# First steps of three stages moved ahead of their stage: embedding spreads, second attention, mixture gate

## The chip, the core and the metric

One Trainium2 chip, of which the kernel uses one core: TensorE (PE; PEld is its weight load), VectorE (DVE), ScalarE (ACT), GpSimd (POOL) and SyncE (SP, which only issues transfers here). Each engine runs its own instruction list in order; the lists meet at semaphores. The metric is the device time of one execution in microseconds (us), the median of several runs. In the rows, L12 is line 12 of the kernel, and a clock of 1.0 or 0.5 is TensorE's granted clock at its full level or at half of it.

## The reference

32 sequences of 512 tokens, width 64. An embedding, then four residual blocks, each on a layer norm of the running state:

```python
h = tok_ref(x, token_W, pe)                      # table row + position row; positions skip pads after a separator
h = h + attn0(layernorm(h), Wq, Wk)              # softmax(q k^T / 8) x, no value or output weights
h = h + ffn0(layernorm(h), route_id, ...)        # 64 -> 128, two layers of shared + routed expert, -> 64
h = h + attn1(layernorm(h), Wq, bq, ..., Wo, bo) # attention with all weights
h = h + ffn1(layernorm(h), Wg, ...)              # 8 experts of 64 -> 128 -> 64 with GELU, sum of the top 2
```

## The kernel before

The state `H` stays on chip for all 32 sequences. A stage handles one sequence per step, with double buffers (`par` is the step's parity), and the stages follow each other: embedding, attention `a0`, routed stage `f0`, attention `a1`, mixture `f1`. Every engine has its own sweep over the sequences; the order of the work on an engine is that of its code, written by hand.

**Embedding.** Token ids become one-hot matrices. On PE `spread_ids(i)` (L909, one 512-column product) spreads the ids of sequence i into bank 2 or 3; DVE compares them with a column (`one_hots`, tile OH, L638). For each four sequences `spread_pos` (L917) and OP (L634) do it for positions. `embed(i)` on PE (L939, L941) is 24 small products of the one-hots with the tables `T3`, each table kept as three bf16 parts; ACT copies the sum to `H` (L413). `embed(i)` waits for OH(i), and behind its products it issues `spread_ids(i + 2)`. DVE has other work between its one-hots: `low_weights` behind sequence 15, `products` behind 20, and a layer norm's statistics (`first_norms`) behind 14, 17, 20, 23 and 26. Ahead of all this, DVE works out positions (L604 to L616), splits the tables into `T3` (L620 to L626), and then spreads the positions (PDX, L589).

**Attention.** For a sequence: PE makes `project` (L1013, L1014) from the turned input X2; ACT copies it (QH, L481); DVE keeps the low part (`low_parts`, Q2, L737); PE makes four 128x512 tiles of scores only to find row maxima (`scores_for_max`, L1024), DVE reduces them (`maxima`, L743); PE spreads the maxima into a row (`spread_max`, L1037), ACT copies it (L497), PE makes the scores again (L1049, L1050), ACT takes exp (L504), PE multiplies with the values (L1058), ACT copies (OT, L475), PE turns back (`turn_back`, L996), and DVE divides and adds to `H` (`finish`, L750 to L754). Inside the sweep, project and maxima of the next sequence run ahead; for sequence 0 they stand ahead of the sweep, one behind the other, and in `a1` behind waits for the routed stage's last step:

```python
if before is not None:
    pe.wait_ge(before.h0_ready, NSEQ)
    pe.wait_ge(before.h1_ready, NSEQ)
    pe.wait_ge(before.h2_ready, NSEQ)
project(0, 0)
...
    rest_before()          # a1: leave0(31), turn_back(31) of the routed stage
for t in range(NT):
    scores_for_max(0, 0, t)
```

**Routed stage.** Per sequence: `enter0` (L1119, L1120), `routed` layer 0 and layer 1 (L1135), with relu on ACT (L530) and on DVE (`layer1`, L797), `leave0` (L1144), a copy on ACT (L473), `turn_back` (L1003) and `add_back` on DVE (L805). The steps of a sequence are spread over several sweep steps, so that after the sweep a tail of layer 1, leave0 and turn_back for the last sequences is left.

**Mixture.** Gate products (`gate_scores`, L1183), the top two on DVE (`copy_xh` L872, `gate_sum` L836 to `gate_masks` L862), turned masks (`turn_masks`, L1190), copied by ACT (`masks`, L547); then eight up products (L1206, L1207), GELU on ACT (L556), and down products (L1226). For sequence 0 the gate's products stand in the last step of `a1`'s sweep, ahead of its values; the choice on DVE (`first_gate`) behind that step's statistics; in the first attention the same two places hold the routed stage's `enter0(0)` and `experts_of(0)`; `turn_masks(0)` on PE and `masks(0)` on ACT behind the attention.

## Time and profile before

| | us |
|---|---|
| median of 3 runs | 935.1 (934.78 to 936.87) |
| the profiled execution | 936.95 |
| span of its instructions | 935.1 |
| PE busy in the span | 891.6 (95%) |
| DVE, ACT, POOL busy | 603.8, 576.6, 384.1 |

The profile was taken in one further execution. Busy times are sums over the span; a PE that is busy may run at half its clock. The stages by the trace: embedding products from 15.3 to 64.6 us, first attention to 287, routed stage to 407, second attention to 632, mixture to the end.

### The profile page before, as it was taken

How to read it: one execution, taken by the hardware profiler on the slowest of the kernel's cores; microseconds unless marked ns; L12 is line 12 of the kernel's file. 1: busy time of each engine (PE TensorE's matmuls, PEld its weight loads, DVE VectorE, ACT ScalarE, POOL GpSimd, SP SyncE). 2: the span in 40 equal slices, each digit the busy share in tenths (PEclk: the TensorE clock that was granted, in tenths of full speed). 3: DMA queues.
4: the chain of work that ended last, by engine and by line, in shares of the span. 5: the costliest groups of instructions: out<-in, count | busy, mean ns of one | idle time of the engine just before them, and what ended most of it. 6: DMA issues, size and time to landing. Idle time of an engine off the chain costs nothing.

```text
span 935.1 us, 21847 instructions
## 1 busy us (share of the span) xinstructions
PE 891.6 (95%) x6198; PEld 631.5 (68%) x6198; DVE 603.8 (65%) x2610; ACT 576.6 (62%) x1195; POOL 384.1 (41%) x523
## 2 busy tenths in 40 slices
PE   4879999999999999979999999999999999999998
PEld 2657666666766676656666676666777777777775
DVE  5876777778787899967777777774434343434321
ACT  1336666666666666646666666666666666666664
POOL 0133444444437888834444344443333333333300
PEclk9999999999999999989999999999999999999999
DMA  4000000000001222200000000000000000000000
GB/s 103 2 1 2 1 0 0 0 0 0 1 1 49 72 73 68 75 7 1 1 0 0 0 0 1 1 1 7 12 18 11 17 11 17 11 17 11 18 13 23
DMA packets 18995, 15.13 MB, mean 16 GB/s; under 512 B 5762, under 2 KB 18946, under 8 KB 18946
## 3 DMA queue, kind: packets, MB, share of 16 engines
q1 hardware_dynamic: 18946, 14.52, 5.6%
q8 instruction: 26, 0.43, 0.2%
q14 instruction: 23, 0.19, 0.1%
HBM read 10.32 MB, written 4.19 MB: 16 GB/s over the span
## 4 chain that ended last, share of the span: by engine, by line
PE 83%; DVE 12%; issue 2%; ACT 1%; DMA 1%; DVEq 0%; POOL 0%; SPq 0%; ACTq 0%
PE bank L1226 13%; PE bank L1058 13%; PE bank L1206 7%; PE bank L1024 7%; PE bank L1207 6%; PE bank L971 5%; DVE nmax L743 5%; PE bank L1049 5%; PE bank L1050 5%; PE bank L1135 4%; PE bank L996 3%; PE bank L1037 2%; PE bank L1013 2%; PE bank L1014 2%; PE bank L1003 2%
## 5 line engine op out<-in xcount | busy, mean ns | idle before, releaser
L743 DVE TENSOR_REDUCE nmax<-bank 128x1 fp32r<-128x512 f32 x256 | 170.4, 687 | 47.7 <-PE bank L1024 47.5
L360 POOL TENSOR_TENSOR XS<-XN,XS 128x252 fp32r<-128x252 f32 x128 | 98.0, 765 | 211.6 <-ACT XS L402 211.6
L342 POOL TENSOR_TENSOR rstd<-VE,half 128x4 f32<-128x4 f32 x128 | 129.2, 1009 | 119.6 <-DVE VE L661 119.6
L504 ACT ACTIVATE PT<-bank 128x512 f32<-128x512 f32 x256 | 146.0, 596 | 41.8 <-PE bank L1050 35.5
L354 POOL TENSOR_TENSOR XN<-XC,rstd 128x252 f32<-128x252 f32 x128 | 78.3, 612 | 183.9 <-PE bank L1058 183.7
L556 ACT ACTIVATE PT<-bank 128x512 f32<-128x512 f32 x256 | 132.2, 605 | 3.5 <-PE bank L1207 2.8
L475 ACT ACTIVATE OT<-bank 128x256 f32<-128x256 f32 x96 | 36.8, 384 | 154.3 <-PE bank L1058 103.8
L1058 PE MATMUL bank<-PT,XN 128*64 128x256 f32 x1024 | 124.7, 386 | 0.0
L1226 PE MATMUL bank<-PT,W 128*64 128x256 f32 x1024 | 124.5, 386 | 0.0
L1024 PE MATMUL bank<-X,QH 128*128 128x512 f32 x256 | 108.2, 424 | 8.6 <-DVE nmax L743 1.7
L1049 PE MATMUL bank<-QH,X 128*128 128x512 f32 x256 | 113.1, 442 | 0.5 <-ACT Q L497 0.5
L453 ACT ACTIVATE X<-bank 128x512 fp32r<-128x512 f32 x128 | 76.1, 595 | 56.7 <-PE bank L971 56.7
L1206 PE MATMUL bank<-X,WH 128*128 128x512 f32 x256 | 107.4, 420 | 0.8 <-ACT K L547 0.8
L1207 PE MATMUL bank<-K,WL 80*128 80x512 f32 x256 | 101.8, 398 | 0.0
L1050 PE MATMUL bank<-Q,X 128*128 128x512 f32 x256 | 101.6, 397 | 0.0
L1058 PEld LDWEIGHTS bank<-PT,XN 128*64 128x64 f32 x1024 | 67.8, 136 | 43.3 <-ACT PT L504 15.5
L1226 PEld LDWEIGHTS bank<-PT,W 128*64 128x64 f32 x1024 | 68.1, 136 | 34.0 <-issue 5.1
L343 POOL TENSOR_TENSOR XC<-H,MV 128x252 f32<-128x252 f32 x128 | 85.1, 665 | 0.0
L836 DVE TENSOR_REDUCE g<-bank 128x32 f32<-128x64 f32 x32 | 7.2, 224 | 118.0 <-PE bank L1183 118.0
L971 PE MATMUL bank<-W,XS 128*128 128x128 f32 x512 | 79.3, 277 | 0.8 <-POOL XS L360 0.8
L647 DVE BATCH_NORM_STATS2 ST<-H 128x6 f32 (+1 forms) x512 | 77.4, 210 | 3.8 <-DVE top L849 1.7
L1024 PEld LDWEIGHTS bank<-X,QH 128*128 128x128 f32 x256 | 48.5, 190 | 45.0 <-DVE nmax L743 36.0
(136 smaller groups left out, 1506.4 us busy)
## 6 DMA issues: line engine op xcount, KB each, us to landing
WR<-experts SPq DMA_DIRECT2D x64, 129.0 KB, 2.0
out<-H SPq DMA_DIRECT2D x32, 128.0 KB, 1.7
W<-pack SPq DMA_DIRECT2D x5, 252.5 KB, 3.9
W<-pack SPq DMA_DIRECT2D x1, 251.5 KB, 5.1
W<-pack SPq DMA_DIRECT2D x1, 243.0 KB, 5.6
tk<-tokens SPq DMA_DIRECT2D x1, 64.0 KB, 4.4
route_sb<-route SPq DMA_DIRECT2D x1, 0.2 KB
```

The source lines that it names most:

```text
L342: pl.tensor_tensor(rstd[:, par, :], VE[:, par, :], half[:, :], ALU.pow).then_inc(sigma_done, 1)
L504: sc_.activation(PT[:, par, kt, :], bank[4 + kt % 2][:, :], ACT.Exp, scale=SCALE).then_inc(s.e_ready, 1)
L556: sc_.activation(G[:, e, :], bank[UP[e % 4]][:, :], ACT.Gelu).then_inc(f1.gelu_ready, 1)
L743: v.tensor_reduce(nmax[:, par, t:t + 1], bank[2 + t % 2][:, :], axis=AX, op=ALU.max, negate=True).then_inc(s.max_ready, 1)
L971: last = nc.tensor.transpose(bank[0][:, t * P:(t + 1) * P], f32(XS[:, par, t, :]), w("ident"))
L1024: mm(bank[2 + t % 2][:, :], QH[:, par, t * P:(t + 1) * P], X2[:, par, :], start=True, stop=True).then_inc(s.s_ps, 1)
L1049: mm(o, X2[:, par, cols], QH[:, par, :], start=True, stop=False)
L1050: mm(o, X2[:, par, cols], Q2[:, par, :], start=False, stop=True).then_inc(s.st_ps, 1)
L1058: last = mm(bank[6][h * D:(h + 1) * D, 0:HALF], XN[:, lane, kt, :], PT[:, par, kt, h * HALF:(h + 1) * HALF], start=(kt == 0), stop=(kt == ...
L1206: mm(o, WH[:, a:a + HID], X2[:, par, :], start=True, stop=False)
L1207: mm(o, WL[0:D + 2 * NEXP1, a:a + HID], K2[0:D + 2 * NEXP1, par, :], start=False, stop=True)\
L1226: last = mm(bank[5 + par][h * D:(h + 1) * D, 0:HALF], w2[:, e, :], G[:, e, h * HALF:(h + 1) * HALF], start=False, stop=(e == NEXP1 - 1))
```

## The change

Five edits. (1) The split of the tables into `T3` moves from DVE to POOL, as the same five instructions, which start when the table transfer has landed; PE's wait counts all five. (2) In `embed(i)`, `spread_ids(i + 2)` and `spread_pos` are issued ahead of the 24 small products. (3) For sequence 0 of the second attention, project, its copy, its low part and the four maxima move into the last step and the tail of the routed stage; their score tiles use banks 5 and 6 for that. The waits for the routed stage's relus then stand behind them. (4) In the last step of the second attention, the mixture's first gate runs early: its products ahead of the last scores, the choice on DVE ahead of `finish` and the statistics, the turned masks ahead of the values; ACT loads the GELU table by a one-column activation (`warm`) behind the last step, then copies the masks, ahead of the last copy of the attention. (5) By the same code the first attention's last step issues `enter0(0)` ahead of its last scores (it stood ahead of the values), and DVE makes the routed stage's first weights (`experts_of(0)`) ahead of `finish(30)`.

On POOL:

```diff
+            pool.wait_ge(head_in, 16)
+            a = at["tok"][0]
+            tables = W[:, a:a + (1 + HOTS) * D].rearrange("p (a d) -> p a d", a=1 + HOTS)
+            pl.memset(w("tok", 1), 0.0).then_inc(parts_ready, 1)
+            pool.wait_ge(parts_ready, 1)
+            pl.tensor_copy(T3[:, :, 0, :], tables).then_inc(parts_ready, 1)
+            pool.wait_ge(parts_ready, 2)
+            pl.tensor_tensor(rest[:, :, :], tables, T3[:, :, 0, :], ALU.subtract).then_inc(parts_ready, 1)
+            pool.wait_ge(parts_ready, 3)
+            pl.tensor_copy(T3[:, :, 1, :], rest[:, :, :]).then_inc(parts_ready, 1)
+            pool.wait_ge(parts_ready, 4)
+            pl.tensor_tensor(T3[:, :, 2, :], rest[:, :, :], T3[:, :, 1, :], ALU.subtract).then_inc(parts_ready, 1)
             pool.wait_ge(consts_set, CONSTS)
```

On ACT:

```diff
             def ffn0(i, par, lane):
                 evac_x_on(f0, a1, i + 2, par)
+                if not has(i + 1):
+                    act.wait_ge(a1.q_ps, 1)
+                    sc_.activation(QH[:, 0, :], bank[1][:, :], ACT.Copy).then_inc(a1.qh_ready, 1)
...
-            attention(a1, f0, f1, 1, lambda: None)
-            masks(0, 0)
+            def first_masks():
+                sc_.activation(warm[:, :], half[:, 0:1], ACT.Gelu)
+                masks(0, 0)
+
+            attention(a1, f0, f1, 1, first_masks)
```

On DVE (the other four instructions of the split go with the first):

```diff
-            link(v.memset(w("tok", 1), 0.0))
...
-                low_parts(0, 0)
-                maxima(0, 0, range(NT))
+                if s is a0:
+                    low_parts(s, 0, 0)
+                    maxima(s, 0, 0, range(NT))
...
                 def body(i, par):
                     if has(i + 1):
-                        low_parts(i + 1, 1 - par)
-                        maxima(i + 1, 1 - par, range(2))
+                        low_parts(s, i + 1, 1 - par)
+                        maxima(s, i + 1, 1 - par, range(2))
+                    else:
+                        meanwhile()
...
-                meanwhile()
                 finish(NSEQ - 1, 1)
...
             add_back(f0, NSEQ - 3)
+            low_parts(a1, 0, 0)
+            maxima(a1, 0, 0, range(2), 5)
             layer1(NSEQ - 1, 1)
             add_back(f0, NSEQ - 2)
+            maxima(a1, 0, 0, range(2, NT), 5)
             add_back(f0, NSEQ - 1)
```

On PE:

```diff
-            pe.wait_ge(parts_ready, 1)
+            pe.wait_ge(parts_ready, 5)
             def embed(i):
                 pe.wait_ge(oh_ready, i + 1)
                 pe.wait_ge(op_ready, q + 1)
+                if i + 2 < NSEQ:
+                    spread_ids(i + 2)
+                if member == 0 and i + HOTS < NSEQ:
+                    spread_pos(q + 1)
...
                 last.then_inc(emb_ready, 1)
-                if i + 2 < NSEQ:
-                    spread_ids(i + 2)
-                if member == 0 and i + HOTS < NSEQ:
-                    spread_pos(q + 1)
...
-                project(0, 0)
                 if before is None:
+                    project(0, 0)
                     turn(s, 1, 1)
-                else:
-                    rest_before()
-                for t in range(NT):
-                    scores_for_max(0, 0, t)
+                    for t in range(NT):
+                        scores_for_max(0, 0, t)
...
                     turn_on(s, after, i + 2, par)
+                    if not has(i + 1):
+                        pe.wait_ge(s.ql_ready, NSEQ)
+                        early()
                     scores(i, par, 0)
...
-                    if not has(i + 1):
-                        pe.wait_ge(s.ql_ready, NSEQ)
-                        meanwhile()
+                    if not has(i + 1) and late is not None:
+                        late()
                     for kt in range(NT):
                         values(i, par, lane, kt)
...
             def ffn0(i, par):
                 turn_on(f0, a1, i + 2, par)
+                if not has(i + 1):
+                    early_project()
...
             leave0(NSEQ - 2, 0)
+            early_scores(0)
+            early_scores(1)
             routed(NSEQ - 1, 1, 1)
             turn_back(f0, a0, NSEQ - 2, 0)
-            def last_turns():
-                leave0(NSEQ - 1, 1)
-                turn_back(f0, a0, NSEQ - 1, 1)
-                pe.wait_ge(f0.ot_ready, NSEQ)
+            early_scores(2)
+            early_scores(3)
+            leave0(NSEQ - 1, 1)
+            turn_back(f0, a0, NSEQ - 1, 1)
...
-            attention(a1, f0, f1, 1, lambda: gate_scores(0, 0), last_turns)
+            attention(a1, f0, f1, 1, lambda: gate_scores(0, 0), lambda: turn_masks(0, 0))
             pe.wait_ge(a1.max_ready, NSEQ * NT)
             pe.wait_ge(a1.e_ready, NSEQ * NT)
-            turn_masks(0, 0)
```

## Rows read from the trace of the kernel before

**Rows 1.** The page's chain that ended last: shares of the span by engine.
```profile
PE 83%; DVE 12%; issue 2%; ACT 1%; DMA 1%; DVEq 0%; POOL 0%; SPq 0%; ACTq 0%
```

**Rows 2.** Stretches: length, busy (x instructions) PE, PEld, DVE, ACT, POOL; clock; DMA; GB/s.
```profile
33.57:63.82 30.25, 21.79 (x443) 17.25 (x439) 24.81 (x87) 8.87 (x22) 9.53 (x13) 0.89 0.01 2
409.50:413.50 4.00, 2.10 (x4) 0.77 (x4) 3.73 (x7) 0.00 (x0) 0.00 (x0) 0.75 0.00 0
411.60:418.30 6.70, 5.92 (x19) 4.17 (x19) 2.58 (x5) 2.43 (x5) 0.00 (x0) 0.50 0.01 2
```

**Rows 3.** Timeline of the head: start, duration, engine, line, operation, out<-in, count, [idle before].
```profile
10.04 0.27 DVE L616 TENSOR_SCALAR posn<-pos 128x128 bf16<-128x128 f32 x1
...
12.38 0.68 DVE L589 TENSOR_TENSOR PDX<-bank,W 128x512 bf16<-128x512 f32 x1
...
15.27 0.32 PE L939 MATMUL bank<-T,OH 128*128 128x64 bf16 x3 [1.55 <-DVE OH L638]
```

**Rows 4.** Groups: POOL by busy, mean ns; one DVE line by min/median/max ns.
```profile
L342 POOL TENSOR_TENSOR rstd<-VE,half 128x4 f32<-128x4 f32 x128 | 129.2, 1009 | 119.6 <-DVE VE L661 119.6
L343 POOL TENSOR_TENSOR XC<-H,MV 128x252 f32<-128x252 f32 x128 | 85.1, 665 | 0.0
L754 DVE TENSOR_TENSOR H<-H,ON x64: 424/425/884, 82.1 to 633.4; 128x256 f32 x44, 128x256 f32<-128x256 f32 x20
```

**Rows 5.** Embedding: PE's waits (us, times, longest), then timeline rows of spreads and what follows.
```profile
PE bank L939 <- DVE OH L638: 10.4, 9, 3.2
...
29.15 0.38 PE L909 MATMUL bank<-IDX,SELB 128*128 128x512 bf16 x1
30.06 0.38 PE L909 MATMUL bank<-IDX,SELB 128*128 128x512 bf16 x1
...
32.40 0.38 PE L909 MATMUL bank<-IDX,SELB 128*128 128x512 bf16 x1
...
39.24 0.26 PE L939 MATMUL bank<-T,OH 128*128 128x64 bf16 x3 [2.73 <-DVE OH L638]
```

**Rows 6.** Timeline: the first attention's last step.
```profile
281.01 0.50 PE L1049 MATMUL bank<-QH,X 128*128 128x512 f32 x1 [0.23 <-ACT Q L497]
```

**Rows 7.** Timeline: the routed stage's tail and the second attention's first step.
```profile
400.61 0.65 PE L1144 MATMUL bank<-F,W 128*64 128x256 f32 x4 [0.44 <-DVE F L797]
...
405.99 0.88 DVE L797 TENSOR_SCALAR F<-bank,WC 128x256 f32<-128x256 f32 x2 [1.48 <-PE bank L1135]
...
407.76 0.65 PE L1144 MATMUL bank<-F,W 128*64 128x256 f32 x4
...
409.46 0.42 DVE L805 TENSOR_TENSOR H<-H,bank 128x256 f32<-128x256 f32 x1 [2.27 <-PE bank L1003]
...
410.60 2.85 DVE L743 TENSOR_REDUCE nmax<-bank 128x1 fp32r<-128x512 f32 x4
...
413.51 0.58 PE L1037 MATMUL bank<-IR,nmax 128*1 128x128 f32 x4 [0.78 <-DVE nmax L743]
...
422.04 0.40 PE L1037 MATMUL bank<-IR,nmax 128*1 128x128 f32 x4
```

**Rows 8.** Timeline: the second attention's end and the mixture's first products.
```profile
628.05 0.18 DVE L750 RECIPROCAL rec<-bank 128x4 f32<-128x4 f32 x1 [1.78 <-PE bank L996]
...
628.85 0.51 PE L1183 MATMUL bank<-GHL,X 128*128 128x16 f32 x4
...
630.66 0.41 DVE L872 CAST K<-X 64x512 fp32r<-64x512 f32 x1
...
631.28 0.38 ACT L475 ACTIVATE OT<-bank 128x256 f32<-128x256 f32 x1 [1.14 <-PE bank L1058]
...
632.59 0.19 DVE L862 TENSOR_SCALAR MK<-took 128x64 bf16<-128x64 f32 x1
...
633.95 1.28 ACT L556 ACT_TABLE_LOAD   x1
...
634.07 0.47 PE L1206 MATMUL bank<-X,WH 128*128 128x512 f32 x1 [0.77 <-ACT K L547]
```

More of the change, by code:

```diff
@@ L211, in tower_kernel @@
         half = sb("half", [P, NT])
+        warm = sb("warm", [P, 1])
         rstd = sb("rstd", [P, 2, NT])
@@ L487, in attention @@
                         embed(i)
-                evac_q(0, 0)
                 if before is None:
+                    evac_q(0, 0)
                     evac_x(s, 1, 1)
@@ L617, in _ @@
                             ALU.add).then_inc(pos_ready, 1)
-            link(v.memset(w("tok", 1), 0.0))
-            a = at["tok"][0]
-            tables = W[:, a:a + (1 + HOTS) * D].rearrange("p (a d) -> p a d", a=1 + HOTS)
-            link(v.tensor_copy(T3[:, :, 0, :], tables))
-            link(v.tensor_tensor(rest[:, :, :], tables, T3[:, :, 0, :], ALU.subtract))
-            link(v.tensor_copy(T3[:, :, 1, :], rest[:, :, :]))
-            v.tensor_tensor(T3[:, :, 2, :], rest[:, :, :], T3[:, :, 1, :], ALU.subtract).then_inc(parts_ready, 1)
             def one_hots(i):
@@ L731, in moments_end_on, with low_parts, maxima @@
                     moments_end(after, s, i - NSEQ, par)
-            def attention(s, before, after, base, meanwhile):
-                def low_parts(i, par):
-                    dve.wait_ge(s.qh_ready, i + 1)
-                    v.tensor_tensor(Q2[:, par, :], bank[1][:, :], f32(QH[:, par, :]),
-                                    ALU.subtract).then_inc(s.ql_ready, 1)
-                def maxima(i, par, tiles):
-                    for t in tiles:
-                        dve.wait_ge(s.s_ps, i * NT + (t + 1))
-                        v.tensor_reduce(nmax[:, par, t:t + 1], bank[2 + t % 2][:, :], axis=AX, op=ALU.max,
-                                        negate=True).then_inc(s.max_ready, 1)
+            def low_parts(s, i, par):
+                dve.wait_ge(s.qh_ready, i + 1)
+                v.tensor_tensor(Q2[:, par, :], bank[1][:, :], f32(QH[:, par, :]),
+                                ALU.subtract).then_inc(s.ql_ready, 1)
+            def maxima(s, i, par, tiles, first=2):
+                for t in tiles:
+                    dve.wait_ge(s.s_ps, i * NT + (t + 1))
+                    v.tensor_reduce(nmax[:, par, t:t + 1], bank[first + t % 2][:, :], axis=AX, op=ALU.max,
+                                    negate=True).then_inc(s.max_ready, 1)
+            def attention(s, before, after, base, meanwhile):
                 def finish(i, par):
@@ L765, in body @@
                     if has(i + 1):
-                        maxima(i + 1, 1 - par, range(2, NT))
+                        maxima(s, i + 1, 1 - par, range(2, NT))
                     moments_on(s, after, i + 5, 1 - par)
@@ L1004, in turn_back, with attention @@
                 last.then_inc(s.back_ps, 1)
-            def attention(s, before, after, layer, meanwhile, rest_before=None):
+            def attention(s, before, after, layer, early, late=None):
                 def project(i, par):
@@ L1150, in _, with early_project, early_scores @@
             pe.wait_ge(a0.e_ready, NSEQ * NT)
+            def early_project():
+                pe.wait_ge(a1.x2_ready, 1)
+                pe.wait_ge(f0.h0_ready, NSEQ)
+                mm(bank[1][:, :], AH[:, 1, :], X2[:, 0, :], start=True, stop=False)
+                mm(bank[1][:, :], AL[:, 1, :], X2[:, 0, :], start=False, stop=True).then_inc(a1.q_ps, 1)
+            def early_scores(t):
+                if t == 0:
+                    pe.wait_ge(a1.qh_ready, 1)
+                if t >= 2:
+                    pe.wait_ge(a1.max_ready, t - 1)
+                mm(bank[5 + t % 2][:, :], QH[:, 0, t * P:(t + 1) * P], X2[:, 0, :],
+                   start=True, stop=True).then_inc(a1.s_ps, 1)
             def ffn0(i, par):
```

## The prediction

> **What bounds the kernel now.** I read the page's chain first, then the stages as stretches with their clock, then the timeline at each seam between stages. The chain is on PE for 83% of the span and on DVE for 12% [rows 1]: inside the stages PE is the bound, and the five edits leave the sweeps alone. What they can win lies where PE waits: in the embedding, where it waits 10.4 us in nine waits for one-hots, and at the seams. A wait costs twice when the clock falls behind it: it is at half for 6.7 us behind the gap at the second attention's start [rows 2].
>
> **Table split on POOL.** DVE ends the positions at 10.31 and starts PDX only at 12.38, the five split instructions lying between; the first small product starts at 15.27 [rows 3]. Without them PDX waits for PE's turn of the positions, some 0.4 us, so at best the start comes 12.38 - 10.7 = 1.7 us earlier, at 13.6. POOL must be done by then. A subtraction there took 0.665 us for 252 columns [rows 4], so 0.84 for 320; two subtractions, two casts at no more than that, a memset and the hops between them are 4 us from about 6.9, so done near 11, under DVE's chain. The casts are not in the trace: at a memset's pace less, at the pace of the power, 1.009 us for 4 columns [rows 4], far more (a rival). What eats this gain is something else: a DVE sum of two operands in SBUF took 0.425 as a median and 0.884 at worst [rows 4], the worst beside a POOL instruction. DVE's position chain has four such instructions, now beside POOL's four. At 0.4 us each all of the gain is gone: 0.1 us left, and I take 0.6, nearer to that end.
>
> The Trainium skill says the same as a rule: "SBUF — State Buffer", section "Who interferes with whom": a VectorE instruction with two SBUF inputs and a GpSimd one that reads SBUF lock each other out for a whole instruction. By that rule alone, applied at each of the four, the gain is 0.1 to 0.2, and the time would be 924.9; the 0.884 of the row agrees with the rule.
>
> **Spreads ahead of the small products.** Today one-hot i+2 can start only when embed(i) is done, so DVE has one embed of time for it, 0.7 us, and each four sequences also a position compare of 0.75. An undisturbed slot is 0.91 us (29.15 to 30.06), but two slots to 32.40 take 2.34, 0.5 more than two of 0.91 [rows 5]. This repeats in each group of four up to sequence 14, about 1.1 us in all. With the spread in front DVE has a whole slot more, and needs 4 x 0.67 + 0.74 = 3.4 of PE's 3.9 us for a group: these waits go. One-hot 14, which now starts on the heels of its spread of 32.40 [rows 5], also starts one embed (0.7) sooner: 1.1 + 0.7 = 1.8 us.
>
> From there to the last one-hot (33.57 to 63.82, 30.25 us) DVE is busy 24.81 [rows 2], with the low parts, the weight sums and five norms between its one-hots, and PE 21.8. So DVE becomes the bound, and what goes is its idle time, 5.4 us, less 0.4 for hops within its chains, 5.0. At the end PE is late: from one-hot 28 it has two slots, a turn of 0.43 and two embeds, 3.7 us, against DVE's 2.0 and the last embed, 2.8: 0.9 back. And the clock: the mean in the stretch is 0.89 [rows 2], that is two falls of about 3.4 us, each behind a hole in which PE waits for DVE's weights (2.73 at 39.24, and the longest, 3.2) [rows 5]. Those holes stay, since DVE's work stays, so I keep both falls. Behind the first, slots of sequence 16 and 17 at half clock and the fused products take 2.3 + 1.6 + 0.9, plus 0.4 for the spread: one-hot 20 could start 5.2 us after one-hot 16, where DVE is ready at 3.9. That is 1.3 back, and 0.1 at the second. The sum is 1.8 + 5.0 - 0.9 - 1.4 = 4.5. If the clock does not fall it is 5.9; if the DVE keeps waiting as now it is nothing. PE's work is the same in number; what stands behind the moved spreads is only embed(i), 0.2 to 0.4 later in its slot.
>
> **First attention's last step.** PE waits 0.23 for ACT ahead of the last scores [rows 6], with about 0.2 of drain; `enter0(0)`, some 0.45 us of PE, fits there and leaves its place ahead of the values. It is two 512-column products, each like the one of that row (0.50, of which they overlap half). The weights on DVE fall into a wait for the turn back like that of the second attention, 1.78 us [rows 8]. The values, the last copy and POOL's next norm come 0.45 earlier; between 0 and 0.5.
>
> **Second attention's start.** Now: relu of layer 1 at 405.99 for 0.88, project, leave0 at 407.76, add_back at 409.46, low part, maxima from 410.60 to 413.45, spread_max at 413.51 [rows 7]. Then: project in the 0.44 us in which leave0 waits for DVE at 400.61 [rows 7], which costs nothing (without that cover 0.45); its copy on ACT delays the next rounding and copy by 0.6, which is 0.9 ahead of its reader. DVE waits 1.48 us ahead of the last relu [rows 7], from 404.51. Into it go the low part (0.65) and two maxima (2.85 / 4, 0.65 back to back; the first waits for its scores until 405.24), so the relu starts at 406.56, 0.57 late, and ends at 407.43. The two score products ahead of the last routed products cost PE 0.43, inside the same 0.57. Leave0 starts at 407.5; from leave0 to add_back's end took 409.88 - 407.76 = 2.12, so the last add_back ends at 409.6. The other two maxima, with add_back(30), run from 407.4 to 409.1 under that. Spread_max needs both, and starts at 409.65 instead of 413.51: 3.86.
>
> The second half is the clock. The first step took 422.04 - 413.51 = 8.53 [rows 7], with 4.8 us at half clock [rows 2], 2.4 too many; at full clock 6.1 to 6.3. PE then has no gap over 0.7 us on the way, where now it is busy for only 2.10 of the 4.00 us ahead of spread_max [rows 2]. So spread_max of sequence 1 comes at 416.0: 6.0 us in all, or 3.9 if the clock falls as long as before, 4.3 for half as long.
>
> **Mixture's start.** The gate's four products go into the wait for ACT (0.05 late). The choice on DVE took 632.78 - 630.66 = 2.1 [rows 8]; the wait of 1.78 ahead of 628.05 shows that DVE is free from 626.27 [rows 8], so it is done at 628.4, before PE ends the last scores at 628.85, where the gate's products now start [rows 8]. `turn_masks` (0.22) takes the place of the gate's products (0.43), and the values end at 631.1 instead of 631.24. `finish(30)` waits 0.4 longer behind the choice, and then POOL's next norm, which the wait for the values covers. ACT is free from 630.14 and idles 1.14 until the values end [rows 8]. Now it loads the table, 1.28 [rows 8], and runs one column (0.2), to 631.65; masks to 632.25; then the last copy (0.38), which now starts at 631.28 [rows 8], to 632.55, 0.9 late. Behind it come turn_back, 0.45 of PE, and the up products, at 633.05 instead of 634.07 [rows 8]: 1.0 us. The fourth up product waits for the last `finish`, near 634.4, when it is due.
>
> The Trainium skill, "ScalarE: Activation LUTs", section "What ACT_TABLE_LOAD costs", gives 2.66 us for a switch, a drain of 1.38 included. By that figure ACT's masks would be done at 633.6, the up products would start 0.3 us later than now, and the time would be 925.7. The trace does not agree here: the load at 633.95 took 1.28 and stands directly behind the copy ahead of it [rows 8], so that case has no chance of its own.
>
> **The rivals.**
> Clock falls again: the three gaps on PE between 407 and 409.7 (0.5, 0.6 and 0.5 us) add up to 1.6. For it: the 4.00 us around the fall now hold 1.9 of idle time, little more [rows 2]; against it: no gap is long. It costs 1.7 to 2.1 us of the 6.0: 926.3.
>
> Embedding gains little: DVE's extra work sets it already, and the clock takes the rest. Then 4.5 becomes 1 at most: 928. For it: the longest single wait, 3.2 us, is DVE's own work. Against it: 5.4 us of DVE idle time in that stretch.
>
> Best case: the clock stays up in the embedding and POOL does not disturb DVE: 1.4 + 1.1 more, 921.9.
>
> Slower: a cast on POOL works at the pace of the power there, 1.009 us for 4 columns. Two casts of 320 columns would take 161 us, and PE waits for all five parts: the first product would start near 171 instead of 14.7, and the time would be some 1,080 us. It decides from the point where the split takes over 14.7 - 6.9 + 12.55 = 20.3 us instead of 4. Subtraction at 0.665 for 252 columns speaks against it.
>
> **How the numbers follow.** 0.6 + 4.5 + 0.45 + 6.0 + 1.0 = 12.55. From the profiled execution, 936.95 (span 935.1), that is 924.4. The profiled execution is 1.85 above the median, and longer than all three runs. A second attention whose clock fell half as long would explain 1.7 of that, but there the gain is smaller by the same: 935.1 - 10.85 = 924.25. So 924.4 stands for the median too. Chances: forecast (922.5 to 925.5 or so) 0.54, clock falls 0.20, embedding gains little 0.13, best case 0.09, slower 0.04. The range, 920.0 to 929.0, takes in the first three with the bounds (embedding 1 to 5.9, split 0.1 to 1.7, seam 3.9 to 6.1) and the best case. A measurement of this kernel tells 0.2% (1.9 us) from no change: faster by more 0.94, within 0.02, slower 0.04.
>
> **What would show it.** Right: spread_max of the second attention some 0.05 behind the last add_back, with no half clock in its first step; the first up product directly behind the last turn_back; DVE without idle time between one-hots 15 and 28. Wrong: the first small product later than 15.27; a PE wait for T3; a second table load; half clock behind the new seam; `turn_masks` waiting for DVE.

## The result, and the profile after

The changed kernel takes 923.09 us as a median (922.11 to 924.56), the kernel before 935.94 (934.78 to 936.87) beside it: a ratio of 0.9865, with an interval of 0.9844 to 0.9885. Faster, and 1.3 us below the forecast of 924.4. The profiled executions, 936.95 and 922.11, lie 14.84 apart and the medians 12.85: the first happened to be the slowest run of its kernel and the second the fastest. On record an execution's time goes with its mean granted clock: of 22 executions of the kernel before in one batch, those at 0.992 to 0.993 took 934.65 to 935.34, those at 0.989 to 0.991 935.95 to 937.47.

Where the spans (935.11 and 920.28) part, by the starts of the same products in both timelines:

| start of | before | after | gained so far |
|---|---|---|---|
| embedding's first small product | 15.27 | 15.07 | 0.20 |
| first attention's first projection | 64.58 | 56.96 | 7.62 |
| its last `spread_max` | 279.92 | 272.74 | 7.18 |
| second attention's first `spread_max` | 413.51 | 402.12 | 11.39 |
| its second `spread_max` | 422.04 | 408.69 | 13.35 |
| its last `spread_max` | 625.29 | 611.65 | 13.64 |
| mixture's first up product | 634.07 | 619.53 | 14.54 |
| end | 935.11 | 920.28 | 14.83 |

On the way through the first attention 0.44 are lost again. In both profiles the clock falls for 3.4 us early in it (at 70.20 and at 61.61); from its first projection to its last `spread_max` it takes 215.34 and 215.78 so, and 214.13 with the spreads alone, where the clock does not fall in it.

The head, against [rows 3]. Timeline of after; the columns are those of [rows 3].

```profile
6.83 0.59 POOL L343 CAST T<-W 128x320 bf16<-128x320 f32 x1
...
7.50 0.89 POOL L345 TENSOR_TENSOR rest<-W,T 128x320 f32<-128x320 f32 x1
7.84 0.69 DVE L628 TENSOR_TENSOR skip<-pad,carry 128x127 f32<-128x127 f32 x1
...
8.98 0.79 POOL L349 TENSOR_TENSOR T<-rest,T 128x320 bf16<-128x320 f32 x1
9.18 0.68 DVE L631 TENSOR_SCALAR kept<-skip 128x128 f32<-128x128 f32 x1
...
10.67 0.27 DVE L635 TENSOR_SCALAR posn<-pos 128x128 bf16<-128x128 f32 x1
...
11.32 0.69 DVE L608 TENSOR_TENSOR PDX<-bank,W 128x512 bf16<-128x512 f32 x1 [0.38 <-PE bank L940]
...
15.07 0.37 PE L959 MATMUL bank<-T,OH 128*128 128x64 bf16 x3
```

POOL's casts are cheap, 0.59 for 320 columns, and its split is done at 9.77. PDX waits 0.38 for PE instead of standing behind the split. But two instructions of DVE's chain for the positions last longer beside POOL, `skip` 0.69 and `kept` 0.68, and the positions end 0.63 later than before. PDX starts 1.06 sooner than at 12.38; 0.24 of that is a table transfer that landed sooner. The first small product gains only 0.20 because a spread of 512 columns and one of the positions now go ahead of it, at 14.27 and 14.65.

The embedding, against [rows 2, 5]: waits (us, times, longest) from 12 to 62 us, then the two timeline rows with the longest holes, then the stretch from the end of one-hot 14 to that of the last one, and the two stretches about the second attention's start, with the columns of [rows 2].

```profile
PE bank L925 <- DVE OH L649: 3.7, 2, 2.1
DVE OH L649 <- PE bank L925: 3.1, 6, 1.4
PE bank L933 <- DVE OH L649: 3.0, 1, 3.0
...
36.46 0.38 PE L933 MATMUL bank<-PDX,SELP 128*128 128x512 bf16 x1 [2.95 <-DVE OH L649]
...
44.48 0.56 PE L925 MATMUL bank<-IDX,SELB 128*128 128x512 bf16 x1 [2.06 <-DVE OH L649]
```

```profile
30.49:55.79 25.30, 19.35 (x444) 16.96 (x449) 23.83 (x87) 8.54 (x22) 9.48 (x13) 0.93 0.01 3
398.12:402.12 4.00, 2.54 (x14) 1.29 (x13) 3.70 (x9) 0.47 (x1) 0.00 (x0) 1.00 0.00 0
...
402.12:408.69 6.57, 6.47 (x39) 4.12 (x40) 4.36 (x15) 4.18 (x8) 0.73 (x1) 1.00 0.01 2
```

PE waits for one-hots three times, for 6.7 us, instead of nine times for 10.4. From the end of one-hot 14 on DVE is busy for 23.83 of 25.30 us, where it was for 24.81 of 30.25 [rows 2]: it sets the pace there, and the two holes that are left stand beside its low weights and weight products. The clock is at 0.93 in this stretch, one fall instead of two. At the second attention's start it is at 1.00, where it was at half for 6.7 us.

One part of this is no wait of PE's. Two additions on DVE (WS, among the `products`) stand beside POOL instructions before, and ahead of them after; timeline rows of before, then of after:

```profile
46.62 0.72 POOL L360 TENSOR_TENSOR XS<-XN,XS 128x252 fp32r<-128x252 f32 x1 [3.98 <-ACT XS L402]
46.88 1.22 DVE L687 TENSOR_TENSOR WS<-WS,W 128x128 f32<-128x128 f32 x2
47.29 0.66 POOL L354 TENSOR_TENSOR XN<-XC,rstd 128x252 f32<-128x252 f32 x1
```

```profile
41.64 0.50 DVE L698 TENSOR_TENSOR WS<-WS,W 128x128 f32<-128x128 f32 x2
42.23 0.72 POOL L373 TENSOR_TENSOR XS<-XN,XS 128x252 fp32r<-128x252 f32 x1 [2.67 <-ACT XS L415]
```

The two took 0.61 and 0.69 before and take 0.29 each now, as in every kernel with the spreads in front: 0.72 us of DVE's time.

The second attention's start, against [rows 7]; timeline rows.

```profile
392.97 0.65 PE L1160 MATMUL bank<-F,W 128*64 128x256 f32 x4
...
396.80 0.69 DVE L746 TENSOR_TENSOR Q<-bank,QH 128x512 fp32r<-128x512 f32 x1
397.73 1.29 DVE L752 TENSOR_REDUCE nmax<-bank 128x1 fp32r<-128x512 f32 x2 [0.25 <-PE bank L1180]
398.93 0.87 DVE L810 TENSOR_SCALAR F<-bank,WC 128x256 f32<-128x256 f32 x2
...
400.04 1.28 DVE L752 TENSOR_REDUCE nmax<-bank 128x1 fp32r<-128x512 f32 x2
401.56 0.42 DVE L818 TENSOR_TENSOR H<-H,bank 128x256 f32<-128x256 f32 x1 [0.23 <-PE bank L1019]
...
402.12 0.40 PE L1053 MATMUL bank<-IR,nmax 128*1 128x128 f32 x4 [0.60 <-DVE H L818]
...
408.69 0.40 PE L1053 MATMUL bank<-IR,nmax 128*1 128x128 f32 x4
```

The low part and two maxima fill DVE's wait ahead of the last relu, the other two run behind it, and `spread_max` now waits for the last `add_back` instead of for maxima. From the same leave0 (400.61 before, 392.97 here) it comes 9.15 us later instead of 12.90.

The mixture's start, against [rows 8]; timeline rows.

```profile
614.49 0.19 DVE L878 TENSOR_SCALAR MK<-took 128x64 bf16<-128x64 f32 x1
...
616.51 1.28 ACT L566 ACT_TABLE_LOAD   x1
617.80 0.20 ACT L566 ACTIVATE warm<-half 128x1 f32<-128x1 f32 x1
618.01 0.59 ACT L562 ACTIVATE K<-bank 24x512 fp32r<-24x512 f32 x1
618.63 0.38 ACT L488 ACTIVATE OT<-bank 128x256 f32<-128x256 f32 x1
...
619.06 0.71 PE L1012 MATMUL bank<-R,OT 128*128 128x130 f32 x4 [1.59 <-ACT OT L488]
619.53 0.48 PE L1239 MATMUL bank<-X,WH 128*128 128x512 f32 x1
```

The masks are chosen before the values begin, and the up products follow the last turn back. The last copy is late instead, behind the table load: PE waits 1.59 for it.

### The profile page after: what moved, and what is told of

The parts are those of the page before. It is cut to its first block, busy times and chain, and to the rows that moved or that the text cites. A ratio compares the mean times of both kernels' runs of the same rounds, so it can differ in the third digit from the quotient of the medians.

```text
span 920.3 us, 21834 instructions
## 1 busy us (share of the span) xinstructions
PE 883.9 (96%) x6184; PEld 627.8 (68%) x6198; DVE 601.5 (65%) x2605; ACT 576.7 (63%) x1196; POOL 386.7 (42%) x528
## 4 chain that ended last, share of the span: by engine, by line
PE 83%; DVE 12%; issue 2%; ACT 1%; DMA 1%; DVEq 0%; POOL 0%; SPq 0%; ACTq 0%
PE bank L1259 13%; PE bank L1074 13%; PE bank L1239 7%; PE bank L1040 7%; PE bank L1240 6%; PE bank L987 5%; DVE nmax L752 5%; PE bank L1065 5%; PE bank L1066 5%; PE bank L1012 3%; PE bank L1151 3%; PE bank L1053 2%; PE bank L1029 2%; PE bank L1030 2%; PE bank L1019 1%
## 5 line engine op out<-in xcount | busy, mean ns | idle before, releaser
L1040 PE MATMUL bank<-X,QH 128*128 128x512 f32 x252 | 105.6, 420 | 7.1 <-DVE nmax L752 0.7
L987 PEld LDWEIGHTS bank<-W,XS 128*128 128x128 f32 x512 | 61.4, 141 | 24.6 <-issue 13.2
```

The lines of the kernel that those rows point to most:

```text
L987: last = nc.tensor.transpose(bank[0][:, t * P:(t + 1) * P], f32(XS[:, par, t, :]), w("ident"))
L1040: mm(bank[2 + t % 2][:, :], QH[:, par, t * P:(t + 1) * P], X2[:, par, :], start=True, stop=True).then_inc(s.s_ps, 1)
```

## The experiments

Theory: the gain is waits taken away, each in its place and independent of the others (embedding some 4.5, second attention's start 3.9, mixture 1.0, split and first attention's end 0.5 each), and the clock at the second attention's start, 2.2. Rivals: the clock alone carries the embedding or the seam; VectorE's work, not the order on PE, bounds the embedding; POOL's port conflicts eat the split. The stretches below, each from timeline rows of a kernel's profile, tell waits from clock: most come out alike in every kernel with the same code there, while the first column and that of the second attention's first step also follow the clock: that step takes 6.55 to 6.57 with no fall, 7.88 to 7.91 with one of 3.4 us and 8.53 to 8.56 with one of 6.8.

| kernel | OP(0) to first projection | first attention's last `spread_max` to values | leave0(29) to second attention's `spread_max` | its first step | its last `spread_max` to up product | up product to end |
|---|---|---|---|---|---|---|
| before | 50.82 | 4.12 | 12.90 | 8.53 | 8.78 | 301.04 |
| spreads alone | 45.13 | 4.10 | 12.60 | 7.89 | 8.79 | 301.03 |
| split alone | 49.84 | 4.10 | 12.61 | 7.88 | 8.79 | 301.05 |
| second attention's start alone | 51.06 | 4.10 | 9.15 | 7.91 | 8.79 | 301.02 |
| gates alone | 50.80 | 3.64 | 12.90 | 8.56 | 7.89 | 300.74 |
| before, idle products at the seam | 50.92 | 4.12 | 13.04 | 6.55 | 8.78 | 303.47 |
| after | 44.25 | 3.65 | 9.15 | 6.57 | 7.88 | 300.75 |
| after again | 44.77 | 3.64 | 9.14 | 6.56 | 7.90 | 300.74 |
| after, no warm activation | 44.78 | 3.64 | 9.15 | 6.56 | 6.79 | 301.02 |
| after, split late | 44.24 | 3.64 | 9.15 | 6.55 | 7.88 | 300.75 |
| after, less DVE work | 43.76 | 3.64 | 9.14 | 7.88 | 7.88 | 300.74 |
| after, idle products in the holes | 44.59 | 3.65 | 9.14 | 7.89 | 7.90 | 300.73 |
| joined | 43.46 | 3.64 | 9.15 | 7.89 | 6.78 | 301.02 |
| joined, warm head | 41.01 | 3.64 | 9.14 | 6.57 | 6.78 | 301.01 |

**The four parts alone**, each on the kernel before. The spreads:

```diff
             def embed(i):
...
+                if i + 2 < NSEQ:
+                    spread_ids(i + 2)
...
                 last.then_inc(emb_ready, 1)
-                if i + 2 < NSEQ:
-                    spread_ids(i + 2)
```

> The kernel before with the second edit alone: the spreads ahead of the small products; the table split stays on DVE. Theory (the waits between PE and DVE in the embedding go, and DVE's own work becomes the bound from sequence 14 on): the first attention's first project comes 5.5 to 7 us earlier than at 64.58, and the time falls by 5 to 7 us. The prediction's own term was 4.5, with both clock falls kept; if it was right and the rest of the embedding's 7.6 us came from the split, the time falls by 4.5 or less. Rival (DVE's extra work sets the embedding anyway): at most 1 us.

Measured: 930.21 against 935.19, ratio 0.9943 (0.9928 to 0.9958). The first projection comes 5.62 sooner. PE still waits 5.9 us for one-hots, in five waits, and the clock falls for 6.8 us in this stretch, as long in all as before. So the order on PE is worth over 5 us with no help from the clock, and the rival in which DVE's work leaves little is out.

The split on POOL:

```diff
-            pe.wait_ge(parts_ready, 1)
+            pe.wait_ge(parts_ready, 5)
...
+            pl.tensor_copy(T3[:, :, 0, :], tables).then_inc(parts_ready, 1)
```

> The kernel before with the first edit alone: the table split on POOL. Theory (DVE's chain is 2.1 us shorter and loses about half of it to POOL's use of the shared port): the position compare and the first one-hot come 0.6 to 1.1 us earlier, and the time falls by about as much. If the port cost nothing: 1.7 us. If it cost all of it: 0.

Measured: 934.5 against 935.19, ratio 0.9992 (0.9983 to 1.0001). OP(0) starts 0.81 sooner; by the interval the time itself can't be told from no change. The 0.98 more up to the first projection (49.84 for 50.82) come where the code is that of before and the clock falls at another place, once for 6.8 us from 47.2 instead of twice for 3.4.

The second attention's start:

```diff
+            low_parts(a1, 0, 0)
+            maxima(a1, 0, 0, range(2), 5)
             layer1(NSEQ - 1, 1)
             add_back(f0, NSEQ - 2)
+            maxima(a1, 0, 0, range(2, NT), 5)
```

> The kernel before with the third edit alone: the first products of the second attention in the routed stage's tail. Theory: spread_max of sequence 0 comes 3.8 us earlier, and its first step takes 6.3 to 6.6 us instead of 8.5 because the clock does not fall: 5.7 us less in the profile. If the clock falls again behind the shorter gaps: 3.8 to 4.3 us less.

Measured: 931.19 against 935.19, ratio 0.9948 (0.9932 to 0.9964). From leave0(29) to `spread_max` it takes 9.15 instead of 12.60 to 12.90, and so in every later kernel. The first step is 7.91 and not 6.56: the clock fell here in spite of the shorter gap. The median gained 4.0, what the expectation gives for a clock that falls again.

The two ends with the early gate and the early weights:

```diff
                 def body(i, par):
...
+                    else:
+                        meanwhile()
...
-                meanwhile()
                 finish(NSEQ - 1, 1)
```

> The kernel before with the last two edits alone, which share their code: the mixture's first gate in the second attention's last step, and the routed stage's first products in the first attention's. Theory: the values of the first attention's last sequence start 0.45 us earlier, and the mixture's first up product 0.45 + 1.0 us earlier: the time falls by 1.2 to 1.6 us. If the table load ahead of the last copy eats what it hides: 0.5 us.

Measured: 934.2 against 935.19, ratio 0.9982 (0.9973 to 0.9992). The first attention's end gives 0.48 (3.64), the mixture's start 0.89 (7.89), and 0.30 more comes behind it (300.74). That is 1.67 in the profile, and 0.99 between the medians, under the 1.2 to 1.6 expected. The four ratios fall short of 1 by 0.0057, 0.0008, 0.0052 and 0.0018, in all 0.0135, as much as the whole change: the parts add up, within the intervals of 0.001 to 0.002 that each has.

**The clock at the second attention's start**, tested on the kernel before with twelve idle products in PE's gap:

```diff
                 for t in range(NT):
                     scores_for_max(0, 0, t)
+                    if before is not None:
+                        filler((0, 5, 1, 6)[t])
```

> The kernel before with twelve idle products, whose results nobody reads, in PE's waits for the maxima at the second attention's start: 5 behind the second score product, 1 behind the third, 6 behind the fourth. No wait is taken away. Theory (of the seam's 5.7 us some 3.8 are waits and some 2 the clock): spread_max of sequence 0 stays behind the last maximum, within 0.1 us, and the first step takes 6.5 instead of 8.5 us, without half clock: 1.2 to 2.0 us less. Rival (the first step is long for another reason, its first-time waits): no change.

Measured: 935.7 against 935.32, ratio 1.0008 (0.9997 to 1.0018). Stretches of this kernel, columns as in [rows 2]:

```profile
411.75:418.45 6.70, 6.61 (x33) 4.48 (x33) 4.08 (x7) 3.92 (x8) 0.73 (x1) 1.00 0.01 2
...
632.60:639.30 6.70, 6.70 (x20) 5.42 (x19) 2.80 (x27) 4.87 (x9) 1.51 (x2) 0.52 0.00 1
```

The clock no longer falls at the seam, and the first step takes 6.55 instead of 8.53. In this profile it falls in the mixture's first step instead, which it had not done in that of before, and the stretch from the first up product to the end is 2.43 longer. The idle products also hold `spread_max` up somewhat, 13.04 behind leave0(29) instead of 12.60 to 12.90. The theory had the mechanism at this place and missed the time: the median gained nothing.

**The embedding's holes**, filled with idle products on the kernel after:

```diff
             for i in range(NSEQ):
+                filler(i, {16: 20, 21: 14}.get(i, 0))
                 embed(i)
```

> The changed kernel with 20 idle products of 128x256 (bf16) in the embedding's first hole and 12 to 14 in its second, while TensorE waits for one-hots; their results are read by nobody. They ask for no more time than the holes have (about 2.2 of 2.95 and 1.5 of 2.06 us at the full clock). Theory (the falls at 44.5 and at 61.6 come because TensorE stands in these holes): one fall or both are gone, the first projection comes up to 1.0 sooner, and the median is 1 to 2 better than the changed kernel's: 921 to 922. Rival (the falls come elsewhere instead, as the idle products at the second attention's start seem to say): the falls' summed length stays, and the median is within 0.5 of the changed kernel's.

Measured: 922.53 against 936.28, ratio 0.9852 (0.9837 to 0.9867); the kernel after beside it has 922.84 and 0.9861. The falls in the embedding and at the first attention's start are gone, but one comes at the second attention's start (7.89). From the low weights on DVE to the first projection it takes 24.20 us instead of 24.76, so the embedding's fall had cost 0.56. In the spreads alone, with a fall of 6.8 us behind the first hole, it takes 25.72: that one cost 1.5. Stretches from the end of one-hot 14 to that of the last one, of the spreads alone and of this kernel, columns as in [rows 2]:

```profile
31.52:57.78 26.26, 21.95 (x452) 18.24 (x449) 23.65 (x88) 8.55 (x22) 9.45 (x13) 0.87 0.01 2
```

```profile
31.32:56.05 24.73, 21.63 (x478) 18.80 (x483) 23.54 (x87) 8.53 (x22) 9.48 (x13) 1.00 0.01 3
```

The median is 0.31 better, within the rival's half a microsecond, but the falls' summed length did not stay as the rival had it: 3.4 us in this profile instead of 6.8.

**VectorE's work in the embedding**, cut:

```diff
+                for k, (low, full, high) in enumerate(lows):
+                    n = 8 if k < 2 else high.shape[-1]
```

> The changed kernel with less work for DVE in the embedding: two of the low-part subtractions behind sequence 15 (0.64 us each) do 8 of their 512 columns, and POOL clears the tile at the start. This leaves out part of the mixture's low weights. Theory (from sequence 14 on DVE is the bound of the embedding): the first attention's first project comes 1.1 us earlier, and the time falls by 1.1 us, or more if the shorter hole keeps the clock up. Rival (PE is the bound, as in the stretch before sequence 14): no change.

Measured: 920.1 against 935.32, ratio 0.9843 (0.9827 to 0.986). DVE is relieved of 1.05 us, and from the low weights to the first projection it takes 23.20 us instead of 24.76: 1.56, of which 0.56 is the fall that is missing in this profile too. The remaining 1.0 is DVE's own time, one for one: in the holes DVE is the bound. Three of the five executions took 919.96 to 920.10 at a mean clock of 0.998 to 1.000, two 923.3 at 0.996, the profiled one among these; so the median shows fewer falls on top of that 1.0.

**The warm activation**, taken out of the kernel after:

```diff
             def first_masks():
-                sc_.activation(warm[:, :], half[:, 0:1], ACT.Gelu)
                 masks(0, 0)
```

> The changed kernel without the one-column activation: ACT copies the masks first, then the last copy of the attention, and loads the table only at the first GELU. Theory (the load ahead of the last copy holds the turn back up by 0.9 us, and a load at the first GELU would be hidden, since PE needs that GELU only four up products and the next gate later): the first up product comes 1.0 us earlier behind the second attention's last spread_max than in the changed kernel (7.0 instead of 8.0 us), and the time is 1.0 us below the changed kernel's. Rival (the early load is what brings the gain): the same as the kernel before at this place, 0.8 us longer than the changed kernel.

Measured: 922.38 against 935.32, ratio 0.9877 (0.9858 to 0.9896). Timeline of ACT and PE:

```profile
617.49 0.59 ACT L562 ACTIVATE K<-bank 24x512 fp32r<-24x512 f32 x1
618.50 0.38 ACT L488 ACTIVATE OT<-bank 128x256 f32<-128x256 f32 x1 [0.43 <-PE bank L1073]
618.90 1.28 ACT L574 ACT_TABLE_LOAD   x1
...
619.41 0.47 PE L1238 MATMUL bank<-X,WH 128*128 128x512 f32 x1
```

The copy no longer waits behind the load, the up products start 1.10 sooner (6.79 instead of 7.90), and the load, now between the copy and the first GELU, gives 0.28 back (301.02). So the early load costs 0.8 net at its place, where it was meant to save. The medians do not show it: 922.38 is 0.5 to 0.7 below the changed kernel's two, but that kernel was not run in the same batch, and by the ratios to the kernel before the order is the other way round, 0.9877 against 0.9861 and 0.9865.

**The split behind the positions**:

```diff
             pool.wait_ge(head_in, 16)
+            pool.wait_ge(pos_ready, 1)
```

> The changed kernel with the table split on POOL started only when DVE has the positions, so that the two no longer overlap. Theory (the shared port costs DVE's position chain 0.85 us): positions end 0.8 us earlier, the position compare as well, and POOL's parts, 2.9 us behind the positions, come just as the first one-hot does, so the first small product comes 0.5 to 0.8 us earlier and the time falls by as much or less. Rival (the chain is later for another reason, such as the landing of the tables): no change, or later by POOL's 2.9 us where the parts are waited for.

Measured: 922.88 against 935.32, ratio 0.9867 (0.9852 to 0.9883). Timeline:

```profile
7.88 0.29 DVE L629 TENSOR_TENSOR skip<-pad,carry 128x127 f32<-128x127 f32 x1
...
8.81 0.22 DVE L632 TENSOR_SCALAR kept<-skip 128x128 f32<-128x128 f32 x1
...
9.85 0.27 DVE L636 TENSOR_SCALAR posn<-pos 128x128 bf16<-128x128 f32 x1
...
10.45 0.45 POOL L344 CAST T<-W 128x320 bf16<-128x320 f32 x1
```

Out of POOL's way `skip` takes 0.29 and `kept` 0.22 again, POOL's cast is faster too, the split still ends ahead of its reader, and the first projection comes 0.83 sooner (56.13). This shows the conflict's price at the head; the median, of four runs, does not show the gain.

**Joined**: the last two, and the part of DVE's work that nobody needs so early put behind the last one-hot.

```diff
+            def late_weights():
...
+                v.tensor_copy(WS[:, :], w("ws"))
                 link(v.tensor_copy(b2h[rows, :], w("b2")[rows, :]))
...
                     first_norms(a0, (i - NORM) // 3)
+            late_weights()
```

> The changed kernel with three things altered, nothing left out: GpSimd's split waits for the positions; the warm GELU activation is taken out again; and of VectorE's work beside the embedding the parts that nobody needs before the routed stage and the mixture (copies of the experts' shared weights with their two additions, 0.69 us, and the b2 rows' cast and two products, 0.95 us) go behind the last one-hot, into VectorE's idle time before the first attention. Theory (VectorE bounds the embedding's two holes, the position chain bounds its start, and the table load is cheapest at the first GELU): the split gives 0.8, the warm activation 0.8 (1.09 earlier at the first up-projection less 0.27 later on), the moved work 0.95 in the first hole and 0.65 in the second, in all 3.2: near 919.9, and the first attention's first projection near 54.5 instead of 56.96. Rival one (once VectorE is relieved, TensorE's own dense work bounds the embedding): the moved work gives under 0.6, 921 or more. Rival two (clock falls take the place of the waits): projection earlier as said, yet the median under 1 us better than the changed kernel's.

> The changed kernel once more, nothing altered, beside the other two, to have its time and its clock on the same chip. Theory (the waits are gone in every run, and what differs from run to run is where the clock falls): first projection at 57.0 within 0.3 of the table's landing, the second attention's first spread 3.7 us sooner behind the routed stage than before, and a median of 922 to 924; the fall at the second attention's start may come back, and then costs 1.3. Rival (the first look was a lucky one): the median is 925 or more.

Measured, side by side: joined 918.57 (917.52 to 921.16), ratio 0.9812 (0.9799 to 0.9826); after again 922.84 (921.92 to 924.44), ratio 0.9861 (0.9846 to 0.9877). The joined kernel is 4.3 us faster than the changed one, with more than the 3.2 expected, and the intervals do not meet. Part of it is fewer clock falls: the joined kernel's executions have a mean clock of 0.996 to 1.000, the other's 0.994 to 0.996, and at 0.996 the one takes 921.16 and the other 921.92 to 922.95. How much is waits and how much clock is not shown. Its profiled execution was the slowest of the five, with the first projection at 55.44 and not 54.5: the small products began at the slow rate that the last experiment is about. The changed kernel again has no fall at the second attention's start, its first projection comes 0.58 later than in the first profile (that slow rate lasts to 17.8 instead of 17.3), and its median agrees within 0.3.

**The slow start of the small products**, with 31 idle products in PE's waits ahead of the embedding, on the joined kernel:

```diff
+            filler(12)
             pe.wait_ge(idx_ready, 1)
...
+            filler(6)
             pe.wait_ge(pdx_ready, 1)
             spread_pos(0)
+            filler(13)
```

> The joined kernel (e9_joined) with 31 idle products of 128x128 (bf16) ahead of the embedding, where TensorE waits: 12 while VectorE writes the ids' mask, 6 while it writes the positions' mask, 13 while the first one-hots are made (about 0.11 us each at the rate that the rows show there, so they end before the waits do). Their results are read by nobody. In all runs so far the first small products go at half their later rate (0.16 us for three instead of 0.087), from 14.3 to 15.3 us until some point between 16.4 and 19.9 us, although the granted clock's row says 1.0 there. Theory (the slow start follows from TensorE's idling ahead of the embedding): the small products go at the full rate from the first one on, the first projection comes 0.9 (from a full rate at 16.4) to 2.0 us (at 18.9, as in the joined kernel's profile) sooner than the 55.44 there, and the median is 0.5 to 1.5 better, near 917.5. Rival (the slow start lasts as long whatever TensorE did, or VectorE's holes take the gain): the projection within 0.4 of what it is without the idle products, the median within 0.4 of 918.6.

Measured: 917.59 (915.76 to 918.34), ratio 0.9801 (0.9787 to 0.9815). First small products, of the joined kernel and then of this one:

```profile
14.35 0.36 PE L963 MATMUL bank<-T,OH 128*128 128x64 bf16 x3
14.53 0.35 PE L965 MATMUL bank<-T,OP 128*128 128x64 bf16 x3
14.69 0.35 PE L963 MATMUL bank<-T,OH 128*128 128x64 bf16 x3
...
18.87 0.25 PE L965 MATMUL bank<-T,OP 128*128 128x64 bf16 x3
```

```profile
13.77 0.25 PE L970 MATMUL bank<-T,OH 128*128 128x64 bf16 x3
13.86 0.25 PE L972 MATMUL bank<-T,OP 128*128 128x64 bf16 x3
13.95 0.25 PE L970 MATMUL bank<-T,OH 128*128 128x64 bf16 x3
```

Three products start every 0.16 us in the joined kernel up to 18.87, and every 0.09 here from the first one on. From the first small product to the first projection it takes 39.03 us instead of 41.09. The median is 0.98 better than the joined kernel's in another batch, inside what the theory named, but the ranges of the runs overlap and so do the intervals of the two ratios: the time does not show the gain.

## Why the prediction was right, step by step

| step | forecast | measured |
|---|---|---|
| split | 0.6 | 0.81 to OP(0); 0.69 between medians, alone |
| embedding's spreads | 4.5 | 5.6 to 5.7 in the profile, 4.98 between medians, alone |
| first attention's end | 0.45 | 0.48 |
| second attention's start, waits | 3.86 | 3.75 in the profile, 3.45 against 12.60 |
| the same, clock | 2.2 | 1.96 in the profile; 1.07 over all profiles |
| mixture's start | 1.0 | 0.89, and 0.30 behind it |

**Split.** The forecast held POOL fast and DVE's chain disturbed, 0.4 us at each of four instructions with two operands in SBUF as the low bound. Of the four only `skip` was, by 0.40: the scan ahead of it takes 0.43 beside POOL and 0.42 before, and the second scan and the sum behind it start when POOL is done (9.77). `kept`, which has one operand and was not among the four, lost 0.46. So 0.81 was left, above the 0.6 taken and below the 1.7 of an undisturbed chain. With the split behind the positions OP(0) starts 5.14 behind the chain's first instruction instead of 6.82 before: that is the 1.7. The rival with a slow cast is out at 0.59. The Trainium skill's rule on the shared ports ("SBUF — State Buffer", "Who interferes with whom"), applied at all four, would have left 0.1 to 0.2: the trace agrees with it in that both engines' instructions lengthen when they meet (POOL's cast 0.45 alone and 0.59 beside DVE), and not in the sum, since of the four only `skip` lost time.

**Spreads.** The mechanism held: from the end of one-hot 14 to the last one DVE is idle for 1.5 us instead of 5.4, and the holes that stay are its own work. The spreads alone have as many us of half clock in the embedding as before, 6.8, and show the terms: 2.1 up to one-hot 14 (forecast 1.8), 4.0 from there to the last one (5.0 less 1.4 for the clock), 0.4 back at the end (0.9). The clock's term was about right for falls of that length: 26.26 against 24.73 without any, so 1.5, and 5.5 without it. In the changed kernel one of the two falls is gone, and the one that is left costs 0.6 (25.30). The other three terms are each 0.3 to 0.5 too low a gain. Not named in the forecast are the 0.72 us of the two additions that no longer stand beside POOL. They hide that, even without a fall, 1.2 us of DVE's idle time stayed in the stretch (24.73 less 23.54), not the 0.4 forecast. This part of the gain is luck.

**Second attention's start.** The waits came out at 3.75 of 3.86, of which 0.30 is there only where the clock had fallen ahead of `spread_max` (12.90 and not 12.60). In the trace of after the three gaps in PE (0.28, 0.57, 0.60) are there as forecast, and the clock stayed up. The rival, that it falls again, came true in some runs: in nine profiles with the new seam the first step took 6.55 to 6.57 five times and 7.88 to 7.91, with a fall, four times; in the four with the old seam and no idle products there it was 7.88 or 7.89 twice and 8.53 or 8.56 twice. The mean goes from 8.22 to 7.15, so the clock's term is 1.07 on average and not 2.2; the forecast took one profile with the longest fall for the rule. The clock's 0.9 and the wait's 0.3 beyond these averages are 1.2 of the 2.0 us by which the profiles differ more than the medians; the other 0.8 is not placed.

**Mixture.** The gain at its place was 0.89. What the forecast did not name is 0.30 behind the first up product; the warm activation alone, in or out, moves that stretch by 0.28 (300.74 and 301.02), so it is the table load that no longer stands ahead of the first GELU. The forecast had the late copy (0.9) and charged it to the load; that leaving the load out is better at this place it did not see.

So the median came out 1.3 us below the forecast. Of this 1.0 is its starting point: it goes down from the profiled execution, 936.95, and the kernel before has a median of 935.94 beside the changed one. The gain itself, 12.85, is 0.3 more than the 12.55 added up: the embedding gave more than its term and the clock at the seam less, and the two misses partly cancel. That the sum comes so near is in part luck. Not settled is which run gets a clock fall where: in both kernels with idle products in waits a fall stands at a place that had none in the profile compared with, but whether it moved there or would have come anyway, and what decides it, is not shown.

## What to carry to other kernels

Cost a wait and the clock behind it separately, and take the clock's part from several profiles: here each wait at a seam was right within 0.4 us, and the clock's part varied by 1.3 us from profile to profile with the same code at that place. Where another engine sets the pace, move that engine's work to where it idles before filling or reordering TensorE: 1.6 us of VectorE's work behind the last one-hot, with two small repairs, brought 4.3 us, a part of them in fewer clock falls. An early table load pays only where ScalarE is free until its next reader: here it delayed a copy on the path by more than it saved.

## What the runs showed of the hardware

In every profile without idle products at the head the first small products ran at half their later rate, three in 0.16 us instead of 0.087, until some point between 16.4 and 20.0 us, which differed between profiles of the same code (17.3 and 17.8 in the two of the changed kernel). The granted clock of the stretch reads 1.00, but the trace holds no record of it there: its first record begins where the slow rate ends, at 17.24 and 17.79 in these two, at 18.83 in the joined kernel. So the slow rate looks like the lower clock level, which no row shows. Thirty-one idle products ahead of them took it away (first record at 13.18), and 2.06 us up to the first projection. Idle products at the second attention's start kept the clock up there, and in that profile a fall of the same length came 220 us later in the mixture; the median gained nothing (ratio 1.0008). While VectorE set the pace, a fall of 3.4 us cost 0.56 and one of 6.8 cost 1.5; at the second attention's start, where TensorE does, 1.3 and 2.0. A POOL cast of 128x320 from f32 to bf16 took 0.45 us alone and 0.59 beside DVE, and a POOL subtraction of that size 0.79 and 0.89.
